# Layer norm scale and shift made from the moments on GpSimd instead of VectorE, in a fused attention and FFN kernel

## What is computed

```
mod = (silu(c) @ wmod).reshape(2, 6, 1, 512)          # sa, ca, ga, sb, cb, gb
ga, gb = magnitude raised to at least 0.25, sign kept
h = layernorm(x) * (1 + ca) + sa                      # (x - mean) / sqrt(var + 1e-5)
Q = relu(rope(h @ W_Q));  H = tanh(Q + hh_b)
o = groupnorm of H, 32 groups of 16 channels, * gn_weight + gn_bias
o = swapaxes(o, -2, -1).reshape(B, T, C)              # transposed rows
x = x + ga * o
h = layernorm(x) * (1 + cb) + sb
g = h @ lut[gate_idx].T;  u = h @ lut[up_idx].T       # 1376 hidden channels
x = x + gb * ((silu(g) * u) @ lut[down_idx].T)
```

## Time and profile before

| what | value |
|---|---|
| median of 3 runs | 1074.4 us (1073.26 to 1078.56) |
| profiled execution | 1077.47 us |
| its span in the trace | 1075.7 us |
| TensorE busy | 973.8 us, 91% |
| VectorE busy | 590.9 us, 55% |
| ScalarE busy | 410.5 us, 38% |
| GpSimd busy | 170.4 us, 16% |

### The profile page before, as it was taken

The page is one execution under the profiler, slowest core; times in us unless marked ns, Lnnn a source line. Parts: engine busy times, 40 slices in busy tenths (PEclk is TensorE's granted clock), DMA queues, the critical chain, the costliest instruction groups (busy, mean ns, idle before and its releaser), DMA issues.

```text
span 1075.7 us, 13315 instructions
## 1 busy us (share of the span) xinstructions
PE 973.8 (91%) x4480; PEld 472.2 (44%) x4480; DVE 590.9 (55%) x1376; ACT 410.5 (38%) x618; POOL 170.4 (16%) x151
## 2 busy tenths in 40 slices
PE   5869669967888989999898899999999999999998
PEld 5534336423333434444444444444444444444443
DVE  5599995875689873334877876322222332222212
ACT  2365764458654632225543531222222321222200
POOL 3111202003456540111201200110000001000000
PEclk9989887988998989999999999999999999999999
DMA  8658353270100011234235214222000112000011
GB/s 291 219 165 215 79 175 89 60 223 2 38 20 30 20 73 55 79 108 118 40 117 156 39 40 157 79 69 88 0 0 0 51 45 102 0 0 0 0 40 40
DMA packets 33737, 83.90 MB, mean 78 GB/s; under 512 B 2976, under 2 KB 2976, under 8 KB 30368
## 3 DMA queue, kind: packets, MB, share of 16 engines
q1 hardware_dynamic: 32544, 75.00, 21.4%
q0 software_dynamic: 1152, 8.39, 4.2%
HBM read 64.50 MB, written 18.87 MB: 78 GB/s over the span
## 4 chain that ended last, share of the span: by engine, by line
PE 69%; DVE 15%; ACT 6%; issue 6%; DMA 2%; SPq 1%; POOL 1%; ACTq 0%; DVEq 0%
PE ps L1089 32%; PE ps L1102 21%; PE ps L1056 7%; PE ps L1078 4%; PE ps L1044 2%; DVE R L802 2%; ACT R L531 2%; PE ps L1115 2%; ACT w_all L522 1%; DVE hid L780 1%; DMA w_all<-wmod_dram 1%; DVE hd L811 1%; PE ps L1068 1%; DMA hid<-idx_dram 1%; DVE xa L791 1%
## 5 line engine op out<-in xcount | busy, mean ns | idle before, releaser
L1089 PE MATMUL ps<-h,w_all 128*128 128x512 f16 x2112 | 468.3, 384 | 18.2 <-DVE hd L811 15.7
L1089 PEld LDWEIGHTS ps<-h,w_all 128*128 (+1 forms) x2112 | 208.0, 99 | 275.4 <-issue 21.1
L1102 PE MATMUL ps<-w_all,hid 128*128 128x512 f16 x1056 | 231.3, 381 | 2.3 <-DVE w_all L979 2.3
L811 DVE SCALAR_TENSOR_TENSOR hd<-ps,col,sg 128x512 f32<-128x512 f32 x88 | 65.9, 749 | 177.9 <-ACT sg L502 177.9
L1102 PEld LDWEIGHTS ps<-w_all,hid 128*128 128x128 f16 x1056 | 103.6, 98 | 127.2 <-DVE w_all L979 2.8
L502 ACT ACTIVATE sg<-ps,col 128x512 f32<-128x512 f32 x88 | 60.1, 683 | 209.0 <-PE ps L1089 208.6
L825 DVE SCALAR_TENSOR_TENSOR hd<-ps,col,gbB 128x512 f32<-128x512 f32 x32 | 24.0, 751 | 155.5 <-PE ps L1102 155.3
L407 POOL TENSOR_TENSOR h<-h,h 128x512 f16<-128x512 f32 x32 | 37.5, 1192 | 395.2 <-ACT h L487 395.2
L507 ACT ACTIVATE hid<-hd 128x512 f32 (+1 forms) x88 | 55.0, 628 | 105.6 <-DVE hd L811 105.6
L1078 PE MATMUL ps<-hid,w_all 128*128 128x512 f16 x352 | 88.6, 415 | 6.5 <-ACT w_all L522 6.5
L1056 PE MATMUL ps<-WQ,work 128*128 128x512 f16 x384 | 89.1, 395 | 4.0 <-DVE col L915 3.1
(11 more groups left out here) (102 smaller groups left out, 762.1 us busy)
## 6 DMA issues: line engine op xcount, KB each, us to landing
R<-x_dram SPq DMA_DIRECT2D x16, 1024.0 KB, 7.0
xa<-x_dram SPq DMA_DIRECT2D x15, 1024.0 KB, 6.4
hid<-idx_dram SPq DMA_DIRECT2D x44, 256.0 KB, 7.2
R<-bias_dram POOLq DMA_DIRECT2D x8, 1024.0 KB, 8.2
out_dram<-R SPq DMA_DIRECT2D x32, 256.0 KB, 2.2
x_dram<-R SPq DMA_DIRECT2D x7, 1024.0 KB, 5.1
w_all<-wmod_dram SPq DMA_DIRECT2D x6, 1024.0 KB, 15.2
h<-idx_dram SPq DMA_DIRECT2D x11, 256.0 KB, 2.6
```

Of the source, the lines that this page charges most:

```text
L811: v.scalar_tensor_tensor(hd[:, s], bank(GU[2 * s + 1]), c_kappa, sg[:, s], ALU.mult, ALU.mult) \
L1089: ins = nc.tensor.matmul(bank(GU[2 * s + t]), W[wp][:, bass.ds(at, P)], h2[hp][:, s, k], start=(k == 0 and i == 0), stop=(k == K - 1 and i ...
L1102: ins = nc.tensor.matmul(bank(QY[par]), hid[hp][:, bass.ds(at, P)], W[wp][:, w_at:w_at + BLK], start=(j == 0 and i == 0), stop=(j == J - 1 ...
```

## The change

VectorE's stats ends with the moments and raises a new semaphore, ln_moments. A new `ln_scale(m)` on GpSimd waits for it and for norm(m - 1) to be done with `ls`, then makes scale and shift in sixteen dependent instructions: add of eps, seed, three times (square, times var, scale and add, times y), mean times y, sign. Each waits for the one before through `pstep`. The last raises ln_stats, for which ScalarE waits as before. VectorE waits for ln_stats before it overwrites `mv`. In GpSimd's list ln_scale(m) stands ahead of split_lo(m), and, in the attention blocks, ahead of the add_bias_rows of the block before.

```diff
+            def ln_scale(m):
+
+                steps = Steps(pool, pstep)
+                steps.base = LN_STEPS * m
+                var, sq_, y, shift_ = (ls[:, i] for i in range(4))
+                pool.wait_ge(ln_moments, m + 1)
+                reach(pool, xn_ready, m)
+                steps.step(nc.gpsimd.tensor_scalar(var, mv[:, :, 1], EPS, None, ALU.add))
+                steps.step(nc.gpsimd.tensor_scalar(y.bitcast(I32), var.bitcast(I32), -0.5, RSQRT_SEED,
+                                                   ALU.mult, ALU.add))
+                for _ in range(3):
+                    steps.step(nc.gpsimd.tensor_tensor(sq_, y, y, ALU.mult))
+                    steps.step(nc.gpsimd.tensor_tensor(sq_, sq_, var, ALU.mult))
+                    steps.step(nc.gpsimd.tensor_scalar(sq_, sq_, -0.5, 1.5, ALU.mult, ALU.add))
+                    steps.step(nc.gpsimd.tensor_tensor(y, sq_, y, ALU.mult))
+                steps.step(nc.gpsimd.tensor_tensor(shift_, mv[:, :, 0], y, ALU.mult))
+                nc.gpsimd.tensor_scalar(shift_, shift_, -1.0, None, ALU.mult).then_inc(ln_stats, 1)
...
+            ln_scale(0)
             split_lo(0, hq[0], hq[1])
             for q in range(NB - 1):
+                ln_scale(q + 1)
                 add_bias_rows(q, 0)
                 split_lo(q + 1, hq[0], hq[1])
             add_bias_rows(NB - 1, 0)
+            ln_scale(LN_B[0])
             split_lo(LN_B[0], h2[0][:, 0], h2[1][:, 0])
+            ln_scale(LN_B[1])
             split_lo(LN_B[1], h2[0][:, 1], h2[1][:, 1])
...
                 if g == 1:
+                    ln_scale(LN_A[NB])
                     split_lo(LN_A[NB], hq[0], hq[1])
                     for n in range(NB, 2 * NB):
+                        if n + 1 < 2 * NB:
+                            ln_scale(LN_A[n + 1])
                         add_bias_rows(n, 1)
                         if n + 1 < 2 * NB:
                             split_lo(LN_A[n + 1], hq[0], hq[1])
                 if g + 1 < G:
                     for s in range(S):
+                        ln_scale(LN_B[(g + 1) * S + s])
                         split_lo(LN_B[(g + 1) * S + s], h2[0][:, s], h2[1][:, s])
...
+                reach(dve, ln_moments, m)
                 for a in range(A):
                     ins = v.bn_stats(st[:, a], x_[:, a])
                 step(ins)
                 alone()
+                reach(dve, ln_stats, m)
                 for a in range(A):
                     ins = v.bn_aggr(mv[:, a], st[:, a])
-                step(ins)
-                reach(dve, xn_ready, m)
-                step(v.tensor_scalar(ls[:, 0], mv[:, :, 1], EPS, None, ALU.add))
-                rsqrt(ls[:, 0], ls[:, 1], ls[:, 2])
-                v.scalar_tensor_tensor(ls[:, 3], mv[:, :, 0], -1.0, ls[:, 2], ALU.mult, ALU.mult) \
-                 .then_inc(ln_stats, 1)
+                ins.then_inc(ln_moments, 1)
```

More of the change, by code:

```diff
@@ L199, in build @@
         id_zero = sem("id_zero"); id_ready = sem("id_ready"); wq_all = sem("wq_all")
-        dstep = sem("dstep")
+        dstep = sem("dstep"); pstep = sem("pstep"); ln_moments = sem("ln_moments")
         silu_c = sem("silu_c"); vec_mm = sem("vec_mm"); row_mm = sem("row_mm")
@@ L219, in build @@
         block = ctx.enter_context(nc.Block())
+        LN_STEPS = 15
         SELECT_AFTER = [u * 7 // 4 for u in range(NCH - SUMMED)]
@@ L401, in _ @@
             nc.gpsimd.partition_all_reduce(c_wqall, c_wqmax, P, RMAX).then_inc(wq_all, 1)
+            def ln_scale(m):
[14 more added lines that the diff above has]
+                nc.gpsimd.tensor_scalar(shift_, shift_, -1.0, None, ALU.mult).then_inc(ln_stats, 1)
+                assert steps.n == LN_STEPS
             def split_lo(m, hi, lo):
```

## The result

The changed kernel takes 1106.8 us (median of 4 runs, 1105.88 to 1110.83) against 1073.8 for the kernel before beside it. The ratio is 1.0315, with a 95% interval of 1.029 to 1.0339: 33.8 us slower. The forecast was 1111, 4 us too high. The profiled execution has a span of 1109.0 us, 33.3 more than that of before.

The account below looks back on a forecast made before the run. The prediction took the norm's latency, not VectorE's busy time, as the bound. Start 5, first batch 9.9, join 8, stats(8) 3.5 and second batch 10.2 sum to 36.6 us, giving 1111 us (range 1092 to 1136).

Parts of the forecast that it names:

- The bound: Attention blocks, first batch: latency releases the norm; VectorE reaches center(3) about 2.3 us sooner but waits for the tanh, gaining nothing.
- The step's price: GpSimd chain of sixteen steps: ten at 0.29 and six at 0.47 us, 5.7 us in all (4.0 to 8.8).
- stats(8): Call ahead of the second batch's attention blocks: the full delay of the norm is paid, 3.5 us.
- d: Delay of the norm after the moments, 5.9 us in place of 2.41: 3.5 us (1.8 to 6.6).
- rival of contention: VectorE and GpSimd exclude each other: about 1.3 us more per block, 12 us in all, 1123; chance 0.2.
- rival of dear steps: Every GpSimd step costs 0.77 us, the chain 12.3: about 1187; chance 0.1 for all above 1136.
- First batch: stats(1) to (3) in attention blocks 0 to 2: delay passed on but for 0.23 us each, 9.9 us.
- Second batch: Three attention blocks with a next norm: affine and product come later, 3 x 3.4 = 10.2 us.
- Join: Attention to FFN: ln_scale(5) stands behind split_lo(4), so norm(5) starts 8 us later (6.5 to 11), all paid.
- Start: ln_scale(0) delays block 0's transposes by 0.8 to 9 us, 5 taken; a second code load: 9, sum 41.
- FFN: Norms of the FFN pairs: the second has 4.3 us of cover, the first far more than the delay; 0 paid.
- Bias rows: Attention block 1: their DMA, issued later behind ln_scale, stays hidden with about 10 us to spare.

Follow-up runs that it names:

- e10: Kernel before, with norm(q + 1) moved behind tanh(3) and the last squares in the first batch, and stats(1) to (3) on GpSimd: 1068.4 us, ratio 0.9951.
- e2: Only stats(1), (2), (3), in the first batch's attention blocks, on GpSimd, against the kernel before: 1079.3 us, ratio 1.0058.
- e3: Only stats(9), (10), (11), in the second batch's attention blocks, on GpSimd, against the kernel before: 1078.4 us, ratio 1.005.
- e5: Only stats(5), the second FFN block at the join, on GpSimd behind split_lo(4), against the kernel before: 1079.7 us, ratio 1.0065.
- e7: The changed kernel with ln_scale(5) ahead of split_lo(4) instead of behind it: 1100.7 us, ratio 1.0236 to the kernel before.
- e6: Only stats(0), the first call, on GpSimd, against the kernel before: 1080.1 us, ratio 1.0071.
- e1: Only the seven calls with cover, stats(4), (6), (7) and (12) to (15), on GpSimd, against the kernel before: 1073.4 us, ratio 0.9999.
- e8: The changed kernel with six steps of Newton instead of three: 1153.3 us, ratio 1.0735 to the kernel before.
- e11: Kernel before, with the next norm behind tanh(3) in both batches' attention blocks and stats(1) to (3), (9) to (11) on GpSimd: 1072.3 us, ratio 0.9996.
- e4: Only stats(8), ahead of the second batch's attention blocks, on GpSimd, against the kernel before: 1077.6 us, ratio 1.0035.

## Why the prediction was right, point by point

**The bound.** Right. I had read that the norm is released by latency and that VectorE's freed time would turn into a wait for the tanh. It did (it is about half of the wait of 4.79 us), and e10 shows the reverse: with that one wait gone, the freed time of three calls is worth 5 us.

**The step's price.** Too high. I took 0.29 us for ten steps and 0.47 for six. Undisturbed, all take 0.28, because a tensor_scalar with constants has none of the 0.39 us that I had extrapolated from forms that read their factors from memory. Undisturbed, the norm starts 4.6 us after the moments (stats(8)), not 5.9. In the blocks it is 5.08, with one step lengthened beside VectorE's L764. So d was 2.2 to 2.7 and not 3.5. The rival of contention exists as a mechanism and costs about 0.45 us per block, not 1.3. The rival of dear steps has no trace here. The step of 0.66 us in each of the six blocks lies beside VectorE's L764, which has two SBUF inputs. The Trainium skill's rule of exclusion (SBUF — State Buffer, section Who interferes with whom) describes this pair. The steps of 0.50 and 0.57 at the start and the join lie beside masks, which have one input; the rule would cover them only in a 2-port mode, and no trace here shows the mode.

**First batch.** 9.9 forecast, 6.2 measured (e2). The term that was mis-sized is d; with 2.7 less 0.2 it gives 7.5.

**Second batch.** 10.2 forecast, 5.4 measured (e3). The delay costs 2.4 us per block and not 3.4, which explains 2.9 us, and 1.6 is the faster projections, a term that I had left out. My claim that TensorE's slack of 1.6 us saves nothing was nearly right: of a delay of 2.7, 2.4 were paid.

**stats(8).** 3.5 forecast, 3.8 measured, right by two errors that cancel: the latency is 2.2 and not 3.5, and 1.3 comes from the matmuls behind the wait, which ran slower and which I had at nothing.

**Join.** 8 forecast, 7.0 measured (e5). Right in mechanism and size, and e7 shows that it is the order.

**Start.** 5 forecast between 0.8 and 9, 7.6 measured (e6). A second empty stretch after the reduction, which I had only as an upper end, is the case: the traces have 5.5 to 6.1 us ahead of the reduction and 7.4 to 8.0 behind it. My 5 was a middle between cases and no working, and I priced this case wrongly: by my own terms one more stretch of 5.73 us gives 0.8 + 5.73 = 6.5, and nothing in the prediction gives the 9. The Trainium skill (GPSIMD Engine Reference, section 2.1, Instruction dispatch) has some 6 us for the first call of a freshly loaded kernel; the traces agree with it ahead of the reduction, and the 9 and the 41 are not its figures. That something stands behind the reduction too, the trace of the kernel before could have told me, by the two configuration instructions at 23.4.

**FFN.** 0 forecast, 0 measured (e1), but by luck. I wrote that the first norm of each pair has far more slack than d, from group 0 alone. In groups 1 and 2 it has 3.0 us, and the change leaves 0.3. With the d that I had forecast, 3.5, it would have cost 0.5 us twice. e8 found this, with an expectation that missed by 12 us.

**Bias rows.** Hidden, as forecast: no wait of the residual names GpSimd or its DMA.

**The sum.** 36.6 forecast, 33.8 measured. The blocks were 8.5 too dear, the start 2.6 and stats(8) 0.3 too cheap, the join 1.0 too dear. The measured parts add to 29.9 and leave 3.9 us to no part. So the total fits better than its terms: that 1111 lies within 4 us of the measured 1106.8 is in part luck. The mechanism (the norm is delayed, and the delay is paid where nothing covers it) is what the experiments bear out.

## What to carry to other kernels

Before moving small work off a busy engine, find who waits for its result and what is queued behind that waiter: here a tanh behind a norm on ScalarE made VectorE's 95% an irrelevant number in the blocks of the first batch, and moving that one norm made the same offload a gain there (in the second batch it did not, e11). On an in-order engine the place in its list can cost more than the arithmetic, as with 7 us for a chain of 4.5 placed behind another block's subtraction. Read the cover of a hidden step in every repetition of it, not only in the first, and test it by making the step longer.

## What the runs showed of the hardware that was not expected

A wait of TensorE can have a second price in the matmuls behind it. 24 matmuls took 5.35 us after an idle of 0.83 (granted clock 1.00), 6.65 after 3.08 (0.80, e4), 8.32 after 3.02 (0.63, the kernel after) and 7.47 after 6.35 (0.70, e8). 16 transposes took 1.91 us without a wait (1.00) and 3.58 after 2.98 (0.50, e8). A clock of 0.50 is 1.2 GHz and 1.00 is 2.4, and the others are stretches with a part at each. The length of the idle alone does not decide it: after an idle of 2.74 us the 48 matmuls of a projection took 12.22 us in one block of the kernel before, and 10.52 after 2.73 in the next.

A GpSimd instruction on 128x4 takes 0.20 us and a dependent one follows at 0.28, against 0.162 and 0.197 on VectorE. The gap of 0.50 us ahead of the affine_select stayed a single case.
